# Gated cross-attention block on one core: another order of TensorE's units in the four kinds of step

## The reference

```python
x = x + tanh(g_xattn) * attention(q=layernorm(x), k=ctx, v=ctx)      # 16 heads of depth 8, softmax over 1601 keys
x = x + tanh(g_ffn) * ffn(layernorm(x))
# ffn: scores = sigmoid(x @ gate_W) * route_scale; the 2 best of 8 experts, their scores divided by their sum
#      expert: gelu(x @ W1 + b1) @ W2 + b2 (hidden 64), plus a shared expert gelu(x @ Ws1 + bs1) @ Ws2 + bs2
```

## Time and profile before

| | |
|---|---|
| median of 3 runs | 1266.49 us (1263.41 to 1267.97) |
| the profiled execution's own time | 1265.94 us |
| its span, first to last instruction | 1263.9 us |
| PE busy | 1182.2 us (94%) |
| DVE busy | 1064.7 us (84%) |
| ACT busy | 1050.4 us (83%) |
| POOL busy | 351.1 us (28%) |

### The profile page before, as it was taken

How to read it: one execution, slowest core, us unless ns; L and a number is a source line. 1 busy time by engine, 2 the same in 40 slices (tenths; PEclk the granted TensorE clock), 3 DMA queues, 4 the chain that set the end, 5 groups by cost and what they waited for, 6 DMA issues and landing times.

```text
span 1263.9 us, 31115 instructions
## 1 busy us (share of the span) xinstructions
PE 1182.2 (94%) x12095; PEld 455.6 (36%) x12095; DVE 1064.7 (84%) x1346; ACT 1050.4 (83%) x1964; POOL 351.1 (28%) x359
## 2 busy tenths in 40 slices
PE   3588999989999999999999999999999999999988
PEld 1223333323334333343333433343333433343325
DVE  6788988989898998989899898989889898989603
ACT  1158889889998899888998899979998898988983
POOL 3461141504242042503424042421424032010100
PEclk7679999999999999999999999999999999999999
DMA  5983536453553555533563645545455525430100
GB/s 152 207 176 82 122 65 140 109 109 95 117 135 70 133 114 110 139 85 98 104 150 80 142 91 121 133 80 122 94 118 131 107 77 121 109 62 17 44 1 18
DMA packets 65572, 132.14 MB, mean 105 GB/s; under 512 B 13713, under 2 KB 40666, under 8 KB 62450
## 3 DMA queue, kind: packets, MB, share of 16 engines
q1 hardware_dynamic: 64494, 129.41, 46.2%
q10 hardware_dynamic: 932, 0.75, 0.2%
HBM read 86.58 MB, written 42.84 MB: 102 GB/s over the span
## 4 chain that ended last, share of the span: by engine, by line
PE 75%; DVE 12%; issue 5%; ACT 3%; SPq 1%; DMA 1%; POOL 1%; POOLq 0%; DVEq 0%; ACTq 0%
PE o_ps L1049 30%; PE a_ps L1031 17%; PE b_ps L1013 13%; DVE run_max L1228 8%; PE a_ps L896 4%; PE a_ps L892 3%; ACT probs L761 2%; PE b_ps L990 2%; PE a_ps L885 2%; DVE run_max L1231 1%; PE b_ps L919 1%; ACT L776 1%; PE a_ps L864 1%; PE a_ps L867 1%; PE a_ps L876 1%
## 5 line engine op out<-in xcount | busy, mean ns | idle before, releaser
L761 ACT ACTIVATE probs<-a_ps 128x512 f32<-128x512 f32 (+1 forms) x1664 | 902.0, 595 | 117.6 <-PE a_ps L1031 103.2
L1228 DVE TENSOR_REDUCE run_max<-b_ps 128x2 f32<-128x1024 f32 x767 | 896.9, 1218 | 104.0 <-PE b_ps L1013 95.8
L1049 PE MATMUL o_ps<-probs,v_op 128*32 128x256 f32 (+1 forms) x5368 | 501.4, 444 | 1.3 <-ACT probs L761 0.6
L1031 PE MATMUL a_ps<-q_op,k_op 51*128 51x256 bf16 (+1 forms) x3328 | 326.9, 275 | 20.9 <-ACT probs L761 15.1
L1013 PE MATMUL b_ps<-k_op,q_op 48*128 48x512 bf16 x2046 | 313.7, 339 | 29.8 <-DVE run_max L1228 24.4
L1031 PEld LDWEIGHTS a_ps<-q_op,k_op 51*128 51x128 bf16 (+1 forms) x3328 | 107.6, 96 | 348.4 <-ACT probs L761 298.4
L1049 PEld LDWEIGHTS o_ps<-probs,v_op 128*32 128x32 f32 x5368 | 107.2, 108 | 185.2 <-issue 112.3
L1013 PEld LDWEIGHTS b_ps<-k_op,q_op 48*128 48x128 bf16 x2046 | 86.7, 94 | 148.6 <-DVE run_max L1228 90.1
L656 POOL TENSOR_TENSOR k_parts<-k_t,one 128x400 bf16<-128x400 f32 (+1 forms) x60 | 51.4, 857 | 226.7 <-ACT k_t L782 225.3
L667 POOL TENSOR_TENSOR rstd_q<-rstd_q,minus_half 128x4 f32<-128x4 f32 x8 | 8.7, 1083 | 281.8 <-DVE rstd_q L1125 281.8
L896 PE MATMUL a_ps<-wv_s,vctx 128*128 128x128 f32 (+1 forms) x416 | 64.3, 294 | 4.5 <-DMA vctx<-ctx_t 4.4
(11 more groups left out here) (129 smaller groups left out, 620.6 us busy)
## 6 DMA issues: line engine op xcount, KB each, us to landing
k_op<-k_dram SPq DMA_DIRECT2D x62, 400.2 KB, 7.1
k_dram<-k_parts SPq DMA_DIRECT2D x30, 600.4 KB, 6.4
vctx<-ctx_t SPq DMA_DIRECT2D x16, 800.5 KB, 4.5
k_op<-k_dram SPq DMA_DIRECT2D x62, 200.1 KB, 7.7
kctx<-ctx_t SPq DMA_DIRECT2D x15, 800.5 KB, 4.8
o_dram<-o_s SPq DMA_DIRECT2D x30, 256.0 KB, 2.1
g_all<-g_dram SPq DMA_DIRECT2D x14, 512.0 KB, 5.8
k_dram<-k_parts SPq DMA_DIRECT2D x30, 200.1 KB, 5.8
```

The source lines that it names most:

```text
L761: act.activation(probs[0:keys, unit % PB, :], a_ps[at % AB][0:keys, :], ACT.Exp, scale=SCALE).then_inc(a_taken, 1)
L1031: last = pe.matmul(a_ps[(at + side) % AB][0:KEYS[t], SEQ * a:SEQ * a + SEQ], k_op[buf][rows, slot, 128 * t:128 * t + KEYS[t]], q_op[buf][r ...
L1049: last = pe.matmul(o_ps[32 * j:32 * j + 32, cols], v_op[s // 2 % 2][0:KEYS[t], t, GP * (s % 2) + j, :], probs[0:KEYS[t], unit % PB, cols], ...
L1228: dve.tensor_reduce(run_max[:, t, :, p, c:c + 1].rearrange("q v o -> q (v o)"), slot[:, :, :], AX.X, ALU.max).then_inc(b_taken, 1)
```

## The change

Only the table `PLAN` changes, so only the order of the units. Per cycle of four steps the counts of units stay as they are (104 `P`, 104 `S`, 64 half and 20 whole `V`, 8 `k`, 8 `v`, 2 `q`, 8 `f`, 4 `y`, 4 `c`, 2 `d`, 4 `T`).

```diff
 PLAN = (
-    "PSVPVSPSkVPSVPSVPSVPSkSPVVPSkSPVVPSVPSVPSVPVSPSkSPVVSPSvPSVVPSTVVPSdPvSPVVPSvPSVVSPSVPVv",
...
-    "PVSPVkSPSkPVVPkVPSVPSVPVPSVPSVPSVPSVPSfVPSVPSVPSVPSVPVSPSfffSSTffSPVdSVPSVPSVPSVPSVPSkSPVV",
...
+    "SPSVVPSkSPVVPSkSPVSPVSPVSPVPSVPSVPSVPSVSPVSPVSPSvSPVVPkSSPVVPSkSPVVPSTdVPSVPSVVPvSPVVP",
...
+    "PSkSPVVPSkkPVVPSVPSVPSkSPVVPSVPSVPSVPSVPSVPSVPSVPSvPVVPSTVVSPvSPSvSPVVPSVPSVSPfVSPVS",
...
```

More of the change, by code:

```diff
@@ L87 @@
 PLAN = (
-    "PSVPVSPSkVPSVPSVPSVPSkSPVVPSkSPVVPSVPSVPSVPVSPSkSPVVSPSvPSVVPSTVVPSdPvSPVVPSvPSVVSPSVPVv",
-    "SSPVVPycPSVVSPyPcSPVVPSycSPVVPSVPSVPSVPSVPSVPSVPSVSPVSPycPSTVVPSVPSVPSVPSVPSfVPSVPSfSPSVV",
-    "PVSPVkSPSkPVVPkVPSVPSVPVPSVPSVPSVPSVPSfVPSVPSVPSVPSVPVSPSfffSSTffSPVdSVPSVPSVPSVPSVPSkSPVV",
-    "PSVPVSSPvqSPVVPSVPVSPSvPSVVPSvPSVVPSVPSVPSVPSvVPSSPVVPSVPSVPSVPSTVSPqSPVVPSVPSVPSVPSV",
+    "SPSVVPSkSPVVPSkSPVSPVSPVSPVPSVPSVPSVPSVSPVSPVSPSvSPVVPkSSPVVPSkSPVVPSTdVPSVPSVVPvSPVVP",
+    "SycfSPSVVPycPSVPSVPSVPSVPSVPSVPSVPSVPycPSVVPSVPSVPSVPSSVPvSPVVPSTVVSPSfPSVPSVPSVVPyPSvcVPSV",
+    "PSkSPVVPSkkPVVPSVPSVPSkSPVVPSVPSVPSVPSVPSVPSVPSVPSVPSvPVVPSTVVSPvSPSvSPVVPSVPSVSPfVSPVS",
+    "PVPSVSvPSVPVSPSfffffSPSVVqdSPVSPVPSVPSVPSVPSVPSVPVSPSVPVSPSTVVPSqSPVSPVPSVPSVPSVPSVPSVPV",
 )
```

## The result

The changed kernel takes 1342.17 us, the median of four runs (1340.57 to 1342.45), against 1264.95 us before (four runs): 77 us more, a ratio of 1.061 with a 95% interval of 1.059 to 1.064. The forecast was 1337 us.

The account below looks back on a forecast made before the run. PE was taken as the bound, busy 143.80 of 146.08 us, with DVE and ACT close behind. To 1265.9 us it added 64 for stalls and 10 for clock, less 3 gained: 1337 us, range 1300 to 1362.

Parts of the forecast that it names:

- The place and the mechanism: First `P` of steps 7 to 31 waits for maxima DMAs queued on SP behind the gates: seven stalls, 64 us.
- The length of a stall: From `FG` to the next step's first `P`: 11.6 us less 2.4 of cover, 9.2 us; bounds 6.2 and 10.8.
- The 2.0 us: Gates' write on SP at the skill's fixed DMA cost instead of 1.40 us: stall 9.8 instead of 9.2 us.
- The clock after a stall: PE behind each of seven stalls: 3.4 us at 1.2 GHz, costing 1.5 us each, 10 us in all.
- The rival of the long spell: Clock stays low longer or gates' write is slow: 10 us stall, 3.5 us clock, 1358 us; chance 0.13.
- The gain of the new order: More even steps across the four phases reclaim some of PE's waits: a gain of 3 us, nearly nothing.
- The bound of 24.4 us: Most that more even steps could reclaim: all `S` units' waits for a `b_ps` slot that DVE still reads.
- The fear that the gates' operations would press on DVE in phase 1: `FL` some twelve units earlier crowds gate operations into five `S`: estimated loss 2 us in each of seven cycles, 14 us.
- The sum: Whole kernel: 1265.9 + 64 + 10 - 3 = 1337 us, from the profiled execution's own time.
- `FT`, `d` and the row of `FH`: `FT` at phase 1's start: 0, at worst 1 us a cycle; `FH` in a row, one phase later: nothing.

Follow-up runs that it names:

- the first experiment: The changed kernel with two statements of SP's step exchanged, the six maxima DMAs issued ahead of the gates' three: 1256.64 us, ratio 0.995.
- the one with the shorter stall: The changed kernel with `FG` nine units earlier in phase 2, SP's order as in the changed kernel: 1322.51 us, ratio 1.047.

## Why the prediction was right, step by step

**The place and the mechanism** were right: seven waits of the first `P` of a phase-3 step for `q_op<-nm_t`, behind `FG`'s copy, the gates' write and the spreads on SP. Three experiments undo or make it alone.

**The length of a stall** was right within 0.6 us: forecast 9.2, measured 8.64 in step 18. Its terms were 1.8 (1.8 measured), 1.4 (1.44), 1.34 (1.34) and 7.0 (6.6), less 2.4 (2.6). The gates' write in the kernel before stood behind six operand loads, four of keys and two of queries, where the prediction counts the four; that changes none of its terms. The 2.0 us that it quotes from the Trainium skill ("DMA: Bandwidth & Descriptors", "Anatomy of one DMA") was measured there on DMAs that GpSimd issues. The write here is issued by SP and took 1.44 us, so the row was the right choice for the sum.

**The clock after a stall** was mis-sized, 1.5 us against 3.67. The forecast took the length of the spell, 3.4 us, from step 2; here the lower clock lasted for about nine us after PE resumed, though PE was busy all the time (4.00 of 4.00 us in the two stretches from 804 to 812). The rival of the long spell named 3.5 us for this term, from the start of step 0, and that was the right row. The page that was cited ("TensorE: Matmul & The Clock Gate" of the Trainium skill) has the direction right, pauses throttle the clock each time: the trace agrees for all seven stalls, 0.56 and 0.50 in the stretches above.

**The gain of the new order** was mis-sized the other way: 3 us forecast; 1.45 us a cycle, ten over seven cycles, of which the ends gave back some, 6.5 us in the total of the first experiment. The bound of 24.4 us was no bound on PE's waits for its partners: it counts the `S` alone, and in the kernel before the `P` waited as well, for ACT. The line of the kernel before, and that of the changed kernel with the exchange:

```profile
PE a_ps L1031 <- ACT probs L761: 15.1, 29, 1.1
```

```profile
PE a_ps L1031 <- ACT probs L761: 10.3, 17, 1.0
```

The `P` gained 4.8 us and the `S` 2.7 (24.4 to 21.7), so the order gained more at the waits that the prediction left out. The fear that the gates' operations would press on DVE in phase 1 was wrong: PE was busy for all 36.51 us of that step. By the strings `FL` stands fifteen units earlier, and not some twelve.

**The sum.** Forecast: 64 + 10 - 3 = 71 us over the profiled 1265.9. Measured by steps: 7 x (8.64 + 3.67 - 1.45) = 76 us, and 77 in the medians. The stall came 4 us short, the clock 16 us over and the order some 7 us under what was written, which leaves 5; the forecast's closeness owes something to these errors' signs.

**`FT`, `d` and the row of `FH`** were costed at nothing, and that holds as far as the list of waits shows it: phases 0 and 1 of the changed kernel take 34.87 and 36.50 us, 0.9 less than before together. The row of `FH` brings one wait of 0.27 us a cycle for the Gelu, 1.6 us in all, and `FT` no new one. What each alone is worth wasn't tried.

## What to carry to other kernels

A table that orders the compute engines also decides when a DMA queue's blocking wait ends, and everything issued behind that wait on the same queue inherits the delay: before moving a unit, look for the queue that waits for its result, and for what stands behind it there. Put what the next stage needs first on the queue, ahead of what it needs only later; here two exchanged statements turn a loss of 6% into a gain of half a percent. Price a stall of TensorE at its length plus the clock's recovery, 3.4 to 5.3 us in this kernel for stalls of 4.9 us and 3.5 to 3.8 for stalls of 8.6, and measure the recovery behind a stall of the same kind.

## What the runs showed of the hardware

- Behind stalls of 4.9 and of 8.6 us step 19 lost the same, 3.8 and 3.7 us; two of the six steps behind the shorter stalls lost 5.3. Matmuls without use in the stall kept the granted clock at 1.00, and the step behind it lost nothing.
- The clock read its lower level, 1.2 GHz, for 8.1 to 13.5 us after PE had taken up its work behind the stalls of the changed kernel and of the one with the shorter stall.
- In the kernel with `FG` in the middle, waits of only 1.15 to 1.79 us were followed by the lower clock and a loss of 4.1 to 4.2 us, more than behind 8.6 us; one of 1.12 us by a loss of 1.5 us, and waits of 0.46 and 0.73 us by none. In the kernel with useless matmuls one of 1.16 us was followed by none. What decides it stays open.
- A 16 KB write to DRAM took 1.44 to 1.51 us until the next issue on a quiet queue (the changed kernel), and 7.2 to 8.2 us half a us behind the operand loads (the kernel before and the one with `FG` in the middle); with the loads nine us old it took 1.6 us.
